# A graph layer on one core: eleven groups of edge rows fetched row by row by two engines, byte offsets made beforehand, and a compare that reads its slot numbers from PSUM

## The reference, cut to what matters

```python
h  = relu(layernorm(x))                                   # 12500 x 128
h1 = concat([h[src], 0, edge_attr]) @ W1 + b1             # 212500 x 256, one row for each edge
h1 = relu(batchnorm(h1))                                  # statistics over all edges
agg = segment_sum(h1, dst) / max(count(dst), 1)           # 12500 x 256
h2 = relu(batchnorm(concat([h, 0, agg]) @ W2 + b2))       # 12500 x 385
out = x + relu(h2 @ W3 + b3)
```

## Time and profile before

| | us |
|---|---|
| median of three runs | 2847.34 |
| the profiled execution's span | 2850.1 |
| table of node rows | 0 to 110 |
| first pass | 110 to 2100 |
| second pass | 2100 to 2740 |
| last node stage | 2740 to 2850 |

### The profile page before, as it was taken

One profiled execution on the slowest core, in us unless ns is written; L12 is line 12 of the kernel. 1 busy time (PEld: TensorE's weight loads), 2 busy tenths in 40 slices (PEclk: granted clock), 3 DMA queues, 4 the chain that ended last, 5 costly groups with the idle time before them and its releaser, 6 DMA issues. The chain is left out here.

```text
span 2850.1 us, 39413 instructions
## 1 busy us (share of the span) xinstructions
PE 2268.9 (80%) x12138; PEld 882.3 (31%) x12138; DVE 1396.5 (49%) x2302; ACT 972.9 (34%) x1601; POOL 1760.7 (62%) x1838
## 2 busy tenths in 40 slices
PE   4687778758777777777777787777779999999989
PEld 4322212212222222222222222222134334444449
DVE  6422222343333333333433333333248998898868
ACT  4422222222222222222222222222235556556546
POOL 7777777777777777777777777777732222222210
PEclk9988888879988899889998888898879999999999
DMA  9677777768777777777777777777749999999956
GB/s 282 212 252 241 246 238 252 258 217 285 239 250 242 245 246 244 239 246 243 256 241 245 244 247 236 250 246 247 232 158 345 350 349 340 342 348 343 341 195 170
DMA packets 273158, 741.18 MB, mean 260 GB/s; under 512 B 47735, under 2 KB 101541, under 8 KB 272944
## 3 DMA queue, kind: packets, MB, share of 16 engines
q1 hardware_dynamic: 192224, 526.86, 52.0%
q0 software_dynamic: 77856, 210.89, 25.2%
q10 hardware_dynamic: 2864, 0.86, 0.2%
HBM read 501.63 MB, written 236.81 MB: 259 GB/s over the span
## 5 line engine op out<-in xcount | busy, mean ns | idle before, releaser
L643 POOL DMA_INDIRECT sums<-P_d,late x1569 | 1506.9, 960 | 479.5 <-issue 466.8
L1379 PE MATMUL psum<-late,sums 128*128 128x512 f32 x1660 | 934.8, 688 | 263.7 <-DVE sums L1080 253.6
L1080 DVE TENSOR_TENSOR sums<-psum,sums 128x1024 f32<-128x1024 f32 x392 | 478.9, 1222 | 1307.7 <-DMA sums<-P_d,late 1283.5
L731 ACT ACTIVATE sums<-sums 128x1024 f32<-128x1024 f32 x416 | 438.8, 1055 | 1510.2 <-DVE sums L1080 1470.0
L1379 PEld LDWEIGHTS psum<-late,sums 128*128 128x128 f32 x1660 | 313.8, 210 | 882.1 <-DVE sums L1080 451.4
L1123 DVE TENSOR_TENSOR late<-late,psum 128x1024 f32<-128x1024 f32 (+1 forms) x407 | 482.2, 1211 | 36.5 <-DMA late<-m_d 34.5
L1322 PE MATMUL psum<-sums,ones 128*32 128x512 f32 x830 | 489.2, 674 | 7.6 <-ACT sums L731 7.6
L1323 PE MATMUL psum<-sums,ones 128*32 128x512 f32 x830 | 489.2, 674 | 0.0
L1324 PE MATMUL psum<-sums,ones 128*32 128x512 f32 x830 | 489.1, 674 | 0.0
L1325 PE MATMUL psum<-sums,ones 128*32 128x512 f32 x830 | 489.1, 674 | 0.0
L672 POOL TENSOR_TENSOR late<-dst_f,iota 128x384 f32<-128x384 f32 (+1 forms) x139 | 115.3, 831 | 379.0 <-PE psum L1491 374.8
(11 more groups left out here) (216 smaller groups left out, 1991.4 us busy)
## 6 DMA issues: line engine op xcount, KB each, us to landing
m_d<-sums SPq DMA_DIRECT2D x415, 512.0 KB
late<-m_d SPq DMA_DIRECT2D x406, 512.0 KB, 5.5
sums<-in_ea_main SPq DMA_DIRECT2D x103, 512.0 KB, 4.4
sums<-P_d,late POOLq DMA_INDIRECT x1569
sums<-P_d SPq DMA_DIRECT2D x1536, 1.0 KB
P_d<-sums SPq DMA_DIRECT2D x24, 512.0 KB, 3.1
nodes<-in_x SPq DMA_DIRECT2D x24, 256.0 KB, 6.5
late<-in_x SPq DMA_DIRECT2D x24, 256.0 KB, 3.2
```

What stands on the lines that cost most here:

```text
L643: pool.indirect_dma_start(out=m_s[s][0:r, k * L:(k + 1) * L], out_offset=None, in_=P1_d, in_offset=bass.IndirectOffsetOnAxis(ap=idx[0:r, G ...
L731: act.activation(q_s[g % Q_SLOTS][0:r, 0:w], m_s[g % M_SLOTS][0:r, 0:w], ACT.Square).then_inc(s_q, 1)
L1080: dve.tensor_tensor(m_s[s][0:r, 0:w], ps_m[place_m[g]][0:r, 0:w], m_s[s][0:r, 0:w], ALU.add).then_inc(s_m, 1)
L1379: ins = pe.matmul(ps_m[place_m[g]][:, 2 * i * L:2 * (i + 1) * L], ea[:, i * P:(i + 1) * P], W1c[:, :], start=True, stop=g not in xg_no, sk ...
```

## The change

- **Rows one by one for eleven whole groups.** Six groups (69, 137, 205, 273, 341, 409) are fetched by SP into `rows_sp`, five (85, 167, 249, 331, 413) by ACT into `rows_act`, all four tiles of each; POOL leaves these groups out altogether. SP takes 64 turns for a group, so two partitions (two register loads, eight DMAs) after each of 64 writes, and then four turns without. ACT takes 80 turns of every 82, one or two partitions after its square.
- **Byte offsets beforehand.** In the table stage DVE shifts the indices of these groups left by ten bits in `idx` (eleven small instructions), and the fetch addresses `P1_d` as bytes, so the register arithmetic before each DMA goes. A plain register copy (`snap`) stands in its place.
- **Slot numbers in PSUM.** DVE copies `iota[:, 0:32]` to PSUM once, and the counting compare reads them there.
- **Space.** The two new buffers take 8 KB of each partition. The scratch in which POOL's DMA descriptors are kept goes from the default to 8192 bytes (`RING`) for it. `by_row` goes.

```diff
-ROWS_FROM = 2
-ROW_GROUPS = 86
+X_FLAT = 18
+SP_ROWS = dict(first=3, turns=64, every=68)
+ACT_ROWS = dict(first=5, turns=80, every=82)
+RING = 8192
...
+        ps_iota = psum[:, 5, 3 * P:3 * P + SPAN]
...
+        def fetch_rows(eng, regs, buf, done, groups, g, first, turns, every):
+            i, n = divmod(g - first, every)
+            if 0 <= i < len(groups) and n < turns:
+                c = GT * groups[i]
+                for p in range(P * n // turns, P * (n + 1) // turns):
+                    eng.load(regs, idx[p:p + 1, c:c + GT])
+                    for k in range(GT):
+                        at = eng.snap(regs[k], min_val=0, max_val=(N - 1) * ROW_BYTES)
+                        row = P1_bytes[bass.ds(at, ROW_BYTES)].rearrange("(a f) -> a f", a=1)
+                        eng.dma_start(buf[p:p + 1, k * L:(k + 1) * L].bitcast(U8), row).then_inc(done[i % 2], 16)
...
             for g in range(NG):
-                if g in xg_no:
+                if g in xg_no or g in rows_at:
                     continue
...
-                for k in range(1 if g in by_row_no else tiles(g)):
+                for k in range(tiles(g)):
...
                 act.activation(q_s[g % Q_SLOTS][0:r, 0:w], m_s[g % M_SLOTS][0:r, 0:w], ACT.Square).then_inc(s_q, 1)
+                if g == ACT_ROWS["first"] and act_rows_at:
+                    act.wait_ge(s_byte, len(rows_at))
+                    table_written(act)
+                fetch_rows(act, row_regs, rows_act, s_row_act, act_rows_at, g, **ACT_ROWS)
...
+            def row_offsets():
+                dve.tensor_copy(ps_iota, iota[:, 0:SPAN])
+                dve.wait_ge(s_idx, 16)
+                for g in rows_at:
+                    c = idx[:, GT * g:GT * (g + 1)]
+                    dve.tensor_scalar(c, c, ROW_BYTES.bit_length() - 1, None, ALU.logical_shift_left).then_inc(s_byte, 1)
...
-                                            iota[:, 0:SPAN].unsqueeze(1).to_broadcast([P, n, SPAN]), ALU.is_equal)
+                                            ps_iota.unsqueeze(1).to_broadcast([P, n, SPAN]), ALU.is_equal)
...
+                elif g in rows_at:
+                    dve.wait_ge(s_mw[s], 16 * (g // M_SLOTS))
+                    dve.wait_ge(s_st, g - M_SLOTS + 1)
+                    if g in sp_rows_at:
+                        dve.wait_ge(s_row_sp[sp_rows_at.index(g) % 2], 16 * GE * (sp_rows_at.index(g) // 2 + 1))
+                        dve.tensor_tensor(m_s[s], ps_m[place_m[g]], rows_sp[:, :], ALU.add).then_inc(s_m, 1)
...
-    nc = bacc.Bacc("TRN2", target_bir_lowering=False, num_devices=1)
+    nc = bacc.Bacc("TRN2", target_bir_lowering=False, num_devices=1, dynamic_dma_scratch_size=RING)
```

More of the change, by code:

```diff
@@ L4 @@
 from concourse import mybir
-F32, I32, U32, BF16 = mybir.dt.float32, mybir.dt.int32, mybir.dt.uint32, mybir.dt.bfloat16
+F32, I32, U32, BF16, U8 = mybir.dt.float32, mybir.dt.int32, mybir.dt.uint32, mybir.dt.bfloat16, mybir.dt.uint8
 ALU, ACT, AX = mybir.AluOpType, mybir.ActivationFunctionType, mybir.AxisListType
@@ L255, in build @@
         xg_b = early(4 * X_GROUPS)
-        by_row = early((GT - 1) * L)
+        taken[0] = max(taken[0], 2 * NPAD - X_FLAT * GE)
         free = [flat[:, a:a + GE] for a in range(taken[0], 2 * NPAD - GE + 1, GE)] + [spare[:, :]]
@@ L300, in build, with row_groups @@
         assert max(ahead_at) < GF - 2 and min(ahead_at) >= AHEAD + 1
[L301 to L304, removed]
+        def row_groups(first, turns, every):
+            return [first + every * (i + 1) - 2 for i in range(GF // every) if first + every * (i + 1) - 2 < GF]
+        sp_rows_at, act_rows_at = row_groups(**SP_ROWS), row_groups(**ACT_ROWS)
+        rows_at = sp_rows_at + act_rows_at
+        assert len(set(rows_at) | set(xg_at)) == len(rows_at) + xg_n
+        rows_sp, rows_act = (sb(n, [P, GT * L]) for n in ("rows_sp", "rows_act"))
+        ROW_BYTES = 4 * L
+        P1_bytes = P1_d.bitcast(U8).rearrange("n f -> (n f)")
+        assert ROW_BYTES & (ROW_BYTES - 1) == 0 and N * ROW_BYTES < 1 << 31
         rng = sb("rng", [P, 2 * GC])
@@ L364, in build @@
         s_ea = [sem(f"s_ea{i}") for i in range(EA_SLOTS)]
-        s_row = [sem(f"s_row{i}") for i in range(len(by_row_at))]
+        s_byte = sem("s_byte")
+        s_row_sp, s_row_act = ([sem(f"{n}{i}") for i in range(2)] for n in ("s_row_sp", "s_row_act"))
         s_eam = sem("s_eam")
@@ L517, in _ @@
                         load_ea(u)
[L519 to L530, removed]
+            row_regs = [sp.alloc_register(f"row_sp{k}") for k in range(GT)]
+            sp.wait_ge(s_byte, len(rows_at))
             table_written(sp)
@@ L548, in _ @@
                     sp.dma_start(rng_row[:, :], range_d.rearrange("(a c) p -> a (c p)", a=1)).then_inc(s_rngl, 16)
-                i, n = divmod(g - ROWS_FROM, ROWS_EVERY)
-                if 0 <= i < len(by_row_at) and n < ROW_GROUPS:
-                    load_rows(i, n)
+                fetch_rows(sp, row_regs, rows_sp, s_row_sp, sp_rows_at, g, **SP_ROWS)
                 for i in ahead_at.get(g, []):
@@ L724, in _ @@
             hT_copy(NB - 1)
+            row_regs = [act.alloc_register(f"row_act{k}") for k in range(GT)]
             for g in range(NG):
@@ L944, in _ @@
                     ln_scale(c)
-            beside = [node_bias, split_destinations]
+            beside = [row_offsets, node_bias, split_destinations]
             for b in range(NB):
@@ L1058, in gathered_before @@
             def gathered_before(g):
-                return 16 * sum(1 if i in by_row_no else tiles(i) for i in range(g % M_SLOTS, g + 1, M_SLOTS) if i not in xg_no)
+                return 16 * sum(tiles(i) for i in range(g % M_SLOTS, g + 1, M_SLOTS) if i not in xg_no and i not in rows_at)
             for g in range(NG):
@@ L1070, in _ @@
                                       b1_bc.unsqueeze(1).to_broadcast([P, GT, L]), ALU.add).then_inc(s_m, 1)
+                elif g in rows_at:
[4 more added lines that the diff above has]
+                        dve.tensor_tensor(m_s[s], ps_m[place_m[g]], rows_sp[:, :], ALU.add).then_inc(s_m, 1)
+                    else:
+                        dve.wait_ge(s_row_act[act_rows_at.index(g) % 2], 16 * GE * (act_rows_at.index(g) // 2 + 1))
+                        dve.tensor_tensor(m_s[s], ps_m[place_m[g]], rows_act[:, :], ALU.add).then_inc(s_m, 1)
                 else:
                     dve.wait_ge(s_gat[s], gathered_before(g))
[L1073 to L1080, removed]
+                    dve.tensor_tensor(m_s[s][0:r, 0:w], ps_m[place_m[g]][0:r, 0:w], m_s[s][0:r, 0:w], ALU.add).then_inc(s_m, 1)
                 if g in ranges:
```

## The result

The changed kernel takes 2932.98 us (median of 4 runs, 2930.97 to 2935.69), the kernel before 2843.36 us (4 runs, 2837.99 to 2848.46). The ratio is 1.0315, with a 95% interval of 1.0296 to 1.0334: slower by 90 us. The forecast was 2877, with a range of 2788 to 2925. The way and the mechanism (SP's queue becomes the bound) came out as forecast; the loss was three times the 30 us forecast.

What follows compares the result with a forecast made beforehand. POOL's gathers were taken to bound the first pass. POOL would gain 56.5 us, but SP becomes the bound and the pass grows by 30: 2850.1 + 30 - 2.8 = 2877 us, range 2788 to 2925.

Steps and rivals of the forecast that it cites:

- What bounded the kernel before: First pass: POOL's 1569 gathers, one every 1.25 us without a pause; 32 fewer save 40 us.
- The compare: Counting compare in the first pass: slot numbers in PSUM stop it slowing POOL's gathers, 16.5 us, bounds 0 and 16.5.
- The order of the queues: First pass: SP replaces POOL as the bound; pass changes by -6 to +67 us, middle +30.
- SP's sum: SP's queue in the first pass: 1925 to 1998 us of work plus 50 of waits, 1975 to 2048 together.
- The price of a partition: SP's row fetches: a four-row partition costs 2.21 us clean, against 1.85 for three rows before.
- The waits that SP cannot avoid: SP's queue in the first pass: 13 us at the start, 24 at six row groups, 13 at the end; 50 together.
- ACT's side: ACT's row fetches in the first pass: 3.5 us a turn, mostly beside the square; taken as 0 us.
- Rival 1: First pass: POOL stays the bound if an SP partition averages 2.14 us or less; 2793.6 us; chance 0.33, whole or part.
- Rival 2: First pass: one DMA engine or the issue itself becomes the bound through single rows; +82 us, 2932; chance 0.10.
- Rival 3: Counting compare still holds POOL up: no change where SP bounds, 2810 us if POOL stays the bound; no chance given.
- The rest at nothing: Twelve small DVE instructions in the table stage, under 4 us, and the halved descriptor space; both taken at nothing.
- The halved descriptor space: POOL's gathers: three or four under way at once, so half the space should not hold POOL up; upper bound unknown.

Runs made afterwards that it cites:

- act_only: The changed kernel with SP's six groups gathered by POOL again and ACT's five kept: 2824.53 us, ratio 0.9932 to the kernel before.
- before_psum: The kernel before with only the slot numbers of the counting compare moved to PSUM: 2829.90 us, ratio 0.9952.
- iota_sbuf: The changed kernel with the slot numbers of the counting compare back in SBUF: 2940.05 us, ratio 1.0319 to the kernel before.
- index_rows: The changed kernel with row numbers for byte offsets, so address arithmetic replaces the register copy before each row: 3004.61 us, ratio 1.0554 to the kernel before.
- sp_only: The changed kernel with ACT's five groups gathered by POOL again and SP's six kept: 2909.17 us, ratio 1.0233 to the kernel before.
- no_copy: The changed kernel without the register copy before each row, on SP and ACT: 2811.43 us, ratio 0.9877 to the kernel before.
- tiny_rows: The changed kernel with each single-row DMA bringing 64 bytes instead of 1024: 2919.73 us, ratio 1.0245 to the kernel before.
- before_ring: The kernel before with only the descriptor scratch halved to 8192 bytes: 2846.46 us, ratio 1.0000.
- five_five: The changed kernel with SP fetching five groups in 80 turns of 82 instead of six: 2825.84 us, ratio 0.9933 to the kernel before.

## Why the prediction was wrong in size and right in kind

**What bounded the kernel before.** Right: gathers on POOL at one every 1.25 us. act_only, with 8 gathers fewer and the compare eased, shortens the pass by 28.6 us; 8 x 1.25 + 16.5 = 26.5.

**The compare.** Forecast 16.5 us for a kernel that POOL bounds; before_psum gave 13.5 on the median, with an interval of 9 to 18. The Trainium skill, in "SBUF — State Buffer", "Who interferes with whom", infers that the generation of DMA descriptors isn't held up by a compare with two SBUF inputs; the row of 1.76 us, before_psum and iota_sbuf speak against that for the gather here. The gather also reads its indices from SBUF, and no run parts that reading from the making of descriptors, so which of the two is held up stays open.

**The order of the queues.** Right: SP becomes the bound, and what POOL gains is given back. SP's wait fell from 761 us to 44 at that line ("under 60"; behind all adds of the pass it is 69), and no gather of 1.7 us is left (longest 1.477). The median two-partition turn is 5.09 us ("4.8 or more"), though clean ones read 4.73. POOL shows 125 us of waits for `m_d` where "some tens" were forecast.

**The step that failed is SP's sum,** 1961 us of work and 50 of waits in the middle forecast, 1993 and 72 in the trace: 54 us too little for the pass (2066 for 2011). The upper end, 1998 and 50, was passed by the waits alone.

*The price of a partition.* Stated: 2.21 us clean, SP's work 1925 us clean and 1998 with the disturbance of the rows before. Measured 1993, 2.30 us a partition. The two parts of the new price came out as taken: 0.024 us off a row (index_rows) for 0.02, and 2.39 - 1.92 = 0.47 us for a fourth row, for 0.44. A clean partition is even cheaper, (4.73 - 0.42) / 2 = 2.155 us, which makes 768 x 2.155 + 228 = 1883 us of clean work. So the disturbance is 110 us, 6% and not 4%. That the work still came out within the bounds is luck: the clean price was too high and the disturbance too low. The middle forecast then took the mean of the clean and the disturbed sum, although the disturbance is in every kernel of this family (in the kernel before it was 37 us); the disturbed value was the one to take. That is 32 of the 54 us.

*The waits that SP cannot avoid.* 50 us forecast, 72 measured, the other 22. The trace shows where they stand (SP's waits by window; the first fence is 121 to 141 us, the second 2160 to 2187):

```profile
SPq L552 <- DVE sums L1107: 13.4, 3, 6.0
```

```profile
SPq L552 <- DVE sums L1104: 17.2, 1, 17.2
SPq L552 <- DVE sums L1107: 5.1, 4, 2.4
SPq L552 <- DVE sums L1101: 1.5, 1, 1.5
```

| | forecast | measured |
|---|---|---|
| start, up to the fifth write | 13 | 15 |
| the six row groups, each with the three writes after it | 24 | 23 |
| the last two writes | 13 | 18 |
| 35 waits of 0.2 to 1.7 us between them | 0 | 15 |

The term at the row groups was right. What was missing is a term for the small waits. They look like a queue with turns of uneven length that now and then catches up with the adds; no run tests that. At the end, "1 to 2 us" was put down for ACT's group 413, where one wait of 17.2 us stands. It was worked out from ACT's average of 3.5 us a turn, with the add of SP's last group in time. That add came late, and behind it ACT has turns of two partitions, 4.9 us (2172.72 to 2177.63) and 5.1.

**ACT's side taken at nothing.** Off by 24 us, the difference between the changed kernel and sp_only; some 12 us of it stand at the end (the last two waits of the pass are 18 us, in sp_only 7), the rest is spread. A partition on ACT takes 2.63 us on average where SP's takes 2.25, a sixth more and not a tenth, from the start of its load to the end of its last DMA. With SP free, in act_only, there is a tail of 7.0 us behind the last gather for 3.1, so part of the end is ACT's own and part comes from SP's late group, which no price of either queue alone shows.

**Rival 1** (POOL stays bound, "a partition at 2.14 or less") had the right point of decision: no_copy is at 2.12 us and POOL-bound. Its profiled execution takes 2802.5 us where 2793.6 was worked out; by medians it is 2811 for 2791. Its pass is 1939 us for 1925, of which POOL's 14.7 us of waits for writes are the most.

**Rival 2** forecast the time that was measured, 2932, by a mechanism that isn't there (and without the 2.8 us that the others take off; with them it is 2929). tiny_rows and no_copy show so: 1/16 of the bytes gives 13 us, one instruction of 34 ns gives 122. Each row does travel in one piece, as the rival supposes: the trace has 5120 packets for ACT's 2560 row DMAs. A rival's number that comes out says nothing for it until something separates it from its neighbour.

**Rival 3** could not show where SP bounds, as said; iota_sbuf agrees. (Its 2810 is without the 2.8 us too. Of the groups up to 406, nine and not ten are fetched by row. Neither touches the forecast.)

**The rest at nothing.** The halved descriptor space: nothing (before_ring). The small DVE work in the table stage: the first gather starts at 113.0 us for 110.6, but in before_ring, which has none of that work, it starts at 112.3; so no cost of it is shown.

## What to carry to other kernels

Work that leaves the busiest engine lands in a queue. Add up that queue's whole time over the stage, at its average and not at its clean price, and compare it with the stage, counting the places where the old bound needs no time but the queue does. Leave it room, as no_copy does (1857 us of work in a pass of 1939, 4%) and five_five (1712 in 1958): a queue whose turn is as long as the old bound's has nothing that absorbs a late one. Measure the last group of the slower helper by itself: what it fetches late stands behind the last gather in every kernel here that leaves group 413 to ACT. When a few instructions are issued thousands of times, look in the trace for those between the ones that were written: here one of 34 ns decided the sign.

## What the runs showed of the hardware

- A single-row DMA on SP costs its issue and not its bytes: 228 ns median for 64 bytes and for 1 KB, and a clean turn of eight of them is 4.73 us with either (tiny_rows and the changed kernel).
- The second single-row DMA after a 128x1024 group write is slower than its neighbours: 368 ns on average in the changed kernel, 338 with rows of 64 bytes, 456 in no_copy, 283 before.
- A register copy of 34 ns costs 44 with its gap (no_copy), the fused arithmetic of 44 ns some 68 (index_rows).
- On ACT the same fetch is dearer than on SP: the load of four registers lasts 587 ns median for 556, the first DMA after it 472 for 268, the others 241 for 228. A partition of four rows takes 2.63 us on average for 2.25.
- A gather that starts inside a DVE compare of two SBUF operands can be held up: the one of 1.76 us for 0.95 ends 0.83 us after the compare. Over all 55 that start inside a compare the mean is 1.25 us. With one operand in PSUM it isn't (58 such gathers of before_psum, mean 0.95). Over the pass this is 32 gathers over 1.2 us against 2, and 13.5 us of 2843.
- Half the descriptor space costs nothing with a gather every 1.25 us (before_ring, 1.0000).
